# The first group of a cross-attention kernel: context turned through TensorE and ScalarE, and one unit's blocks moved per head

## What is computed

```
q = norm(x) @ Wq            # 16 heads of 128
k, v = ctx @ Wk, ctx @ Wv   # ctx: 2 x 2048 tokens x 128; 8 kv heads, each for 2 q heads
p = softmax(q k^T / sqrt(128), with a key mask)
x = x + (p @ v) @ Wo
```

## Time and profile before

| | |
|---|---|
| median of 3 runs | 354.47 us (354.44 to 355.21) |
| the profiled execution | 353.88 us |
| its span | 352.1 us |
| PE busy | 329.0 us, 93% |
| DVE, ACT, POOL busy | 278.7, 231.5, 244.9 us |

### The profile page before, as it was taken

One profiled execution on the slowest core, in us unless ns is written; L12 is line 12 of the kernel. 1 busy time (PEld: TensorE's weight loads), 2 busy tenths in 40 slices (PEclk: granted clock), 3 DMA queues, 4 the chain that ended last, 5 costly groups with the idle time before them and its releaser, 6 DMA issues.

```text
span 352.1 us, 6886 instructions
## 1 busy us (share of the span) xinstructions
PE 329.0 (93%) x2231; PEld 297.1 (84%) x2231; DVE 278.7 (79%) x472; ACT 231.5 (66%) x410; POOL 244.9 (70%) x150
## 2 busy tenths in 40 slices
PE   6875699999999999999999999998989999888996
PEld 4664599999999999999999988997878897588995
DVE  4599877988988989889889889735568844579997
ACT  4487577687677777777767687973246675257762
POOL 4839499599599599599598499778154868434550
PEclk9999989999999999999999999999999999999999
DMA  7705886886895895895795796693034040403630
GB/s 199 243 25 132 203 194 150 204 198 140 205 205 129 206 206 126 207 207 126 179 203 118 169 218 171 161 314 94 8 89 151 0 149 4 149 14 90 189 112 31
DMA packets 33332, 52.07 MB, mean 148 GB/s; under 512 B 5792, under 2 KB 23328, under 8 KB 33312
## 3 DMA queue, kind: packets, MB, share of 16 engines
q1 hardware_dynamic: 33312, 51.82, 58.9%
HBM read 20.08 MB, written 0.26 MB: 58 GB/s over the span
## 4 chain that ended last, share of the span: by engine, by line
PE 69%; DVE 8%; POOL 7%; issue 5%; ACT 4%; SPq 3%; DMA 3%; DVEq 0%; POOLq 0%; ACTq 0%
PE bank L554 11%; PE bank L555 11%; PE bank L556 10%; PE pair L554 10%; PE pair L556 10%; PE pair L555 10%; POOL pT L417 3%; POOL ctx_lo L417 3%; SPq L262 3%; DMA ctx_raw<-in_ctx_dram 2%; POOL ctxT_lo L417 2%; PE bank L801 1%; PE pair L793 1%; PE bank L832 1%; DVE resid L1680 1%
## 5 line engine op out<-in xcount | busy, mean ns | idle before, releaser
L417 POOL TENSOR_TENSOR pT<-pT,pT_hi 128x1024 fp32r<-128x1024 f32 x60 | 143.0, 2409 | 38.7 <-ACT pT_hi L1056 38.5
L1046 ACT ACTIVATE probs<-probs,lowest 128x2048 f32<-128x2048 f32 x32 | 64.2, 2007 | 23.6 <-DVE lowest L1366 23.5
L1056 ACT ACTIVATE pT_hi<-pT 128x1024 fp32r<-128x1024 f32 x60 | 61.6, 1052 | 16.2 <-DMA pT<-blocks 14.1
L555 PE MATMUL bank<-pT,ctx_hi 128*128 128x256 f32 x240 | 69.0, 288 | 0.0
L554 PE MATMUL bank<-pT_hi,ctx_lo 128*128 128x256 f32 x240 | 68.7, 286 | 0.0
L556 PE MATMUL bank<-pT_hi,ctx_hi 128*128 128x256 f32 x240 | 68.4, 285 | 0.0
L554 PE MATMUL pair<-ctxT_hi,qk_lo 128*128 128x512 f32 x128 | 51.7, 404 | 5.7 <-DVE qk_lo L1322 2.5
L1366 DVE CUSTOM_DVE_ANT_0 probs<-pair,mask_bias,lowest 128x1024 f32<-128x1024 f32 x32 | 41.0, 1281 | 12.7 <-PE pair L556 11.8
L556 PE MATMUL pair<-ctxT_hi,qk_hi 128*128 128x512 f32 x128 | 50.4, 394 | 0.0
L555 PE MATMUL pair<-ctxT_lo,qk_hi 128*128 128x512 f32 x128 | 50.3, 393 | 0.0
L554 PEld LDWEIGHTS bank<-pT_hi,ctx_lo 128*128 128x128 f32 x240 | 45.7, 191 | 1.5 <-POOL pT L417 0.5
(11 more groups left out here) (236 smaller groups left out, 810.8 us busy)
## 6 DMA issues: line engine op xcount, KB each, us to landing
pT<-blocks SPq DMA_DIRECT2D x128, 128.0 KB, 2.3
pT<-ctx_raw SPq DMA_DIRECT2D x112, 128.0 KB, 2.3
ctx_raw<-ffn_experts_gate_up_dram SPq DMA_DIRECT2D x16, 256.0 KB, 2.9
wq<-in_L_xattn_Wq_dram SPq DMA_DIRECT2D x8, 256.0 KB, 2.6
ctx_raw<-in_ctx_dram SPq DMA_DIRECT2D x8, 256.0 KB, 6.5
wo<-in_L_xattn_Wo_dram SPq DMA_DIRECT2D x8, 256.0 KB, 3.0
blocks<-in_L_attn_w_q_dram SPq DMA_DIRECT2D x4, 512.0 KB, 4.0
blocks<-in_L_attn_w_dense_dram SPq DMA_DIRECT2D x4, 512.0 KB, 4.4
```

Of the source, the lines that this page charges most:

```text
L417: pool.tensor_tensor(dst, src, hi.bitcast(F32), ALU.subtract).then_inc(ready, 1)
L555: pe.matmul(dst, w[0], x[1], start=False, stop=False)
L1046: act.activation(probs[:, j], probs[:, j], ACT.Exp, bias=lowest[:, p, j, 1:2], scale=-1.0, accum_out=den[:, p, j:j + 1]).then_inc(exps, 1)
L1056: act.activation(hi_slot(c), chunk(p, c).bitcast(F32), ACT.Copy).then_inc(pT_hi_ready, 1)
```

## The change

The turned context of p = 1 (chunks 4 to 7) is no longer made from the raw chunks with a DVE subtraction. ACT rounds the raw chunk, POOL takes its rest, then PE transposes the hi part and the lo part separately (`ctx_part`, eight pieces in the order of `PARTS`), and ACT copies each out of PSUM. For this, `ctx_round` of chunks 4 to 7 comes before that of 2 and 3, and POOL's rests become eight pieces of 512 columns, four of them ahead of `rest_wq(1)` and of the second mask. The second mask is loaded into the bytes of `wo`, so `load_o(0)` waits behind both masks and moves behind the moves of unit 0. `q_fold(0)` comes before the fourth chunk. In the first group the blocks of unit 0 move head by head: 16 DMAs of 32 rows x 2 KB for head 0 once it is turned, `load_wk(2)`, then 16 for head 1. The counts of `landed[0]` shift by 256.

```diff
+        PARTS = ((0, 0), (0, 1), (0, 2), (1, 0), (1, 1), (0, 3), (1, 2), (1, 3))
...
+        def move(eng, p, a, q, heads=slice(0, J)):
+
+            eng.dma_start(pT[p][LN * q:LN * (q + 1), a, heads].bitcast(F32),
+                          blocks[p][LN * a:LN * (a + 1), q, heads]).then_inc(landed[p], 16)
...
+            load_wq(1)
+            load_wk(1)
             load_mask(1)
-            load_o(0)
...
-            load_wq(1)
-            load_wk(1)
...
             load_wq(2)
-            move_blocks(0, 0)
-            load_wk(2)
+            for j in range(J):
+                sp.wait_ge(turned, j + 1)
+                for r in range(QD):
+                    for q in range(QD):
+                        move(sp, 0, q, (q + r) % QD, slice(j, j + 1))
+                if j == 0:
+                    load_wk(2)
+            sp.wait_ge(mask_ready, B * NCH)
+            load_o(0)
             load_wq(3)
...
+            def ctx_rest(b, k, rounded):
+                pool.wait_ge(ctx_hi_ready, rounded)
+                part, cols = slice(4 * k, 4 * k + 4), slice(b * KEYS + k * CH, b * KEYS + (k + 1) * CH)
+                rest(ctx_lo[:, b, part].rearrange("p i d -> p (i d)"), ctx_raw[:, cols],
+                     ctx_hi[:, b, part].rearrange("p i d -> p (i d)"), ctx_lo_ready)
...
             mask(0)
+            for k in range(NCH):
+                ctx_rest(1, k, 3 + k)
+            rest_wq(1)
             mask(1)
-            rest_wq(1)
-            ctx_rest(0)
-            ctx_rest(1)
+            for k in range(NCH):
+                ctx_rest(0, k, B * NCH)
...
+            def ctx_part(n):
+
+                lo, k = PARTS[n]
+                if lo:
+                    pe.wait_ge(ctx_lo_ready, k + 1)
+                else:
+                    pe.wait_ge(ctx_hi_ready, k + 3)
+                if n < 2:
+                    pe.wait_ge(ctxT_lo_ready, n + 3)
+                elif n == 2:
+                    pe.wait_ge(qk_lo_ready, 2)
+                else:
+                    pe.wait_ge(parts_ready, n - 2)
+                for i in range(4):
+                    last = pe.transpose(PART_BANK[n % 3][:, i * P:(i + 1) * P],
+                                        (ctx_hi, ctx_lo)[lo][:, 1, 4 * k + i].bitcast(F32), ident[:])
+                last.then_inc(parts_psum, 1)
...
+            score(0, 0)
+            ctx_part(0)
+            pe.wait_ge(ctxT_lo_ready, NCH)
+            score(0, 1)
+            ctx_part(1)
+            score(0, 2)
+            score(0, 3)
+            for n in range(2, 7):
+                ctx_part(n)
+            q_project(1, 0)
+            q_project(1, 1)
+            ctx_part(7)
+            pe.wait_ge(parts_ready, 5)
+            score(0, 4)
+            pe.wait_ge(parts_ready, 8)
+            score(0, 5)
+            wk_transpose(1)
...
             fold_copy(0, 1)
-            ctx_chunk(4)
-            ctx_chunk(5)
+            ctx_round(4)
+            ctx_round(5)
+            ctx_part(0)
+            ctx_part(1)
+            ctx_round(6)
+            ctx_round(7)
+            wq_round(1)
             exp_row(0, 0)
-            ctx_chunk(6)
-            ctx_chunk(7)
-            wq_round(1)
+            ctx_part(2)
+            ctx_part(3)
             exp_row(0, 1)
-            for c in range(1, B * NCH):
-                ctx_round(c)
+            for n in range(4, 8):
+                ctx_part(n)
+            ctx_round(2)
+            ctx_round(3)
```

More of the change, by code:

```diff
@@ L183, in perceiver_layer @@
         D_LAST = (bank[7], bank[1])
-        CTX_BANK = [bank[i] for i in (2, 3, 4, 5, 4, 5, 4, 5)]
+        CTX_BANK = [bank[i] for i in (2, 3, 4, 5)]
+        PART_BANK = bank[4:7]
+        PARTS = ((0, 0), (0, 1), (0, 2), (1, 0), (1, 1), (0, 3), (1, 2), (1, 3))
         TURN_BANK = [bank[i] for i in (7, 6, 0, 1, 7, 6, 0, 1)]
@@ L220, in perceiver_layer @@
         ctx_hi_ready, ctx_lo_ready = sem("ctx_hi_ready"), sem("ctx_lo_ready")
+        parts_psum, parts_ready = sem("parts_psum"), sem("parts_ready")
         wv_hi_ready, wv_ready, wo_hi_ready, wo_ready = (
@@ L258, in perceiver_layer @@
         stored = sem("stored")
-        def move(eng, p, a, q):
-            eng.dma_start(pT[p][LN * q:LN * (q + 1), a].bitcast(F32),
-                          blocks[p][LN * a:LN * (a + 1), q]).then_inc(landed[p], 16)
+        def move(eng, p, a, q, heads=slice(0, J)):
+            eng.dma_start(pT[p][LN * q:LN * (q + 1), a, heads].bitcast(F32),
+                          blocks[p][LN * a:LN * (a + 1), q, heads]).then_inc(landed[p], 16)
         block = stack.enter_context(nc.Block())
@@ L308, in _, with move_blocks @@
                          ).then_inc(ld_gate, 16)
-            load_wq(1)
-            load_wk(1)
-            def move_blocks(g, p):
+            def move_blocks(g, p, rounds=range(QD)):
                 after(sp, av, 4 * (2 * g + p - 1))
                 sp.wait_ge(turned, 2 * (2 * g + p) + 2)
-                for r in range(QD):
+                for r in rounds:
                     for q in range(QD):
@@ L338, in _ @@
                     load_o(g)
-            sp.wait_ge(landed[0], 256 * G)
+            sp.wait_ge(landed[0], 256 * (G + 1))
             def load_qkv(r):
@@ L689, in _ @@
             ctx_chunk(2)
+            q_fold(0)
             ctx_chunk(3)
[L691 to L705, removed]
+            pe.wait_ge(ctxT_lo_ready, 2)
+            score(0, 0)
[15 more added lines that the diff above has]
+            wk_transpose(1)
+            score(0, 6)
+            score(0, 7)
+            q_fold(1)
             for m in range(BEATS):
                 if m == 2:
-                    pe.wait_ge(ctx_lo_ready, 1)
-                if m == 6:
-                    pe.wait_ge(ctx_lo_ready, B)
+                    pe.wait_ge(ctx_lo_ready, B * NCH)
                 beat(1, m, True, False, True)
@@ L982, in ctx_chunk, with ctx_part @@
                 act.activation(ctxT_hi[:, b, k * CH:(k + 1) * CH], CTX_BANK[c][:], ACT.Copy).then_inc(ctxT_hi_ready, 1)
+            def ctx_part(n):
+                lo, k = PARTS[n]
+                act.wait_ge(parts_psum, n + 1)
+                act.activation((ctxT_hi, ctxT_lo)[lo][:, 1, k * CH:(k + 1) * CH], PART_BANK[n % 3][:],
+                               ACT.Copy).then_inc(parts_ready, 1)
             def ctx_round(c):
@@ L1052, in p_round @@
                 if c == 0:
[L1053 removed]
+                    act.wait_ge(landed[p], 256 * (g + 2 - p))
                 after(act, av, 4 * (u - 1) + c + 1 if not isinstance(u, int) or u else 0)
@@ L1115, in _ @@
             ctx_chunk(1)
+            ctx_round(1)
             ctx_chunk(2)
@@ L1375, in turn @@
                 if j == 0:
-                    after(dve, landed[p], 256 * g)
+                    after(dve, landed[p], 256 * (g + (0 if isinstance(g, int) and g == 0 else 1 - p)))
                 dve.transpose(blocks[p][:, :, j].rearrange("p q k t -> p k q t"),
@@ L1493, in _ @@
             ctx_chunk(3)
+            fold_rest(0, 1)
             dve.wait_ge(mask_ready, 2)
@@ L1497, in _ @@
             dve.wait_ge(mask_ready, 4)
[L1498 to L1507, removed]
+            for m in range(1, 4):
+                mask_pair(0, m)
             turn(0, 0)
             turn(0, 1)
+            dve.wait_ge(mask_ready, 6)
             mask_pair(0, 4)
+            dve.wait_ge(mask_ready, B * NCH)
             mask_pair(0, 5)
-            any_key(1)
             q_rest(1)
@@ L1517, in _ @@
             fold_rest(1, 0)
-            dve.wait_ge(ctxT_psum, B * NCH)
             dve.wait_ge(ctx_hi_ready, B * NCH)
-            dve.wait_ge(ctx_lo_ready, B)
+            dve.wait_ge(ctx_lo_ready, B * NCH)
             turn(0, 2)
             turn(0, 3)
+            for p in range(B):
+                any_key(p)
             group(1, True, False)
```

12 lines of the change are left out of this document (3 added, 9 removed).

## The result

The changed kernel takes 363.41 us (median of 4 runs, 362.67 to 363.70) against 354.46 for the kernel before in the same session: a ratio of 1.0249, interval 1.0216 to 1.0281. It is 9.0 us slower; the prediction said 5.3 slower and a range that ended at 361.5. The profiled execution took 362.67, its span is 360.9 instead of 352.1: +8.8 to be explained, where the sum said +5.6. It is the fastest of the four; the median lies 0.7 us above it, as 0.6 was forecast.

The account below looks back on a forecast made before the run. PE's own work bounds the kernel from group 1 on, so only group 0's delay counts: first attend 49.5 plus 1.7 slow clock, 51.2 against 45.5, is +5.6 on 353.9. Named: 359.8 us, range 352.0 to 361.5.

Parts of the forecast that it names:

- the sum: Whole kernel: first attend at 51.2 in full-speed terms against 45.5 before, +5.6 us.
- The step on which all hung: Unit 0's moves in group 0: 64 KB moves issue every 0.635 us, like 128 KB ones.
- T: Group 0: start of ACT's rounding of unit 0's blocks, 45.9 instead of 40.75; first attend 3.55 us later.
- The slow clock: PE's cold restart after its hole before the first attend: 1.7 us charged, the same as before.
- The end of unit 1: Second unit's moves: piece 0 ready at 61.7, before PE gets there at 63.3, so nothing is added.
- What the rebuild frees: Group 0, POOL, DVE and PE: context rests end at 32.0 instead of 36.0; PE could attend from 40.8.
- T = 26.25 + 31 s: Unit 0's moves start at 23.45; 32 issues at pitch s, 0.635 us, put ACT's rounding at 45.9.
- Nothing else in the diff touches a later group: Groups from 1 on: unaffected except for the order of two loads, which was taken to cost nothing.
- PE without holes from then on: Sign expected in the profile after: PE runs without a hole once past its first attend near 49.5.
- The full price: Unit 0's moves at a pitch of 0.59 to 0.64 us: +4.5 to +5.8, or 1.7 less if clock holds; chance 0.48.
- the late rebuild: Rival, group 0: ping-pong between PE and ACT turns head 0 a us late, +1 on any case; chance 0.06.

Follow-up runs that it names:

- the moves alone: The kernel before, with only the first unit's moves split by head; 363.68 us, ratio 1.0270.
- half the bytes: The changed kernel with only the first half of unit 0's key blocks moved in group 0, 32 moves of 32 KB; 361.43 us in one execution.
- whole moves: The changed kernel with unit 0's blocks moved as before, 16 moves of 128 KB; 353.83 us against 354.16, ratio 1.0004.
- two queues: The changed kernel with eight of head 1's moves issued by ACT instead of SP; 358.65 us in one execution.
- one turn written out on the changed kernel: The changed kernel with one turn of PE's loop (group 2) written out by hand, same work in more instructions; 364.57 us in one execution.
- two turns written out: The changed kernel with 128 KB moves, second mask in `ones`, and groups 2 and 3 of PE's loop written out; 351.93 us against 354.23, ratio 0.9932.

## Why the prediction was wrong, point by point

**Direction and main mechanism: right.** The step on which all hung, that 64 KB moves are issued at the pitch of 128 KB ones, is shown three times: 0.63 us each in the moves alone and at half the bytes, and the moves' whole time is cut only by a second issuing engine. From T to the first attend it is 51.26 - 47.72 = 3.54 us, as taken. The slow clock cost 1.5 us behind the first attend where 1.7 was charged; that this was close is in part luck, since the run of the moves alone paid 2.9 us after a hole of nearly the same length. The end of unit 1 added nothing.

**What the rebuild frees: right, but each step came about 1 us later.** POOL's last context rests ended at 33.1 (32.0 forecast), heads 2 and 3 were transposed from 33.99 to 38.4 (33.2 to 37.7), wk's transpose came at 40.20 (39.3). Score 2 ended at 42.0, when PE's hole begins (40.8). None of this was on the path that decided. With whole moves PE was through with score 2 at 41.3 and attended at 42.15, 3.3 us earlier than before, where the prediction's 40.8 would have made it 4.7.

**T = 26.25 + 31 s: the first step that failed, too small by 1.8 us.** T was 47.72, not 45.9. SP started at 24.40, not at 23.45. This start varies: it is 23.57, 23.45 and 23.47 in the runs with half the bytes, with two queues and with one turn written out on the changed kernel, and in those PE's wait for the context chunks was shorter too; so 0.9 us of it belong to this execution and not to the rebuild. How usual such a start is stays open, since the other three executions of the changed kernel were longer still. The other part is that s was taken as the same for all 32 moves: one issue of the first sixteen took 1.71 us instead of 0.59, at 28.2, with a q8 packet at 28.0 beside it (11.23 us for 16, but 10.00 for the next 16). The landing, 2.0 us instead of 2.2, gave 0.2 back. The earlier trace rows shows nothing of the kind, its longest issue is 0.708: in the kernel before that packet comes at 24.3, ahead of the first move at 28.73. The change starts the moves 4.3 us sooner, and its packet falls among them; in the three other runs named here the issue beside it took 1.13 to 1.45 us.

**"Nothing else in the diff touches a later group": the second step that failed.** It is true of the code and false of the time. The rebuild makes TensorE's program longer, which moves the fetch packet of the last groups from a unit where it cost 0.6 us to one where it cost 1.9: 1.3 us. This is shown by the run that writes out one turn in the kernel before (a hole appears), and by the one that writes out two (it goes); that the packet is TensorE's follows from these and from the matmul counts, not from a label in the trace. The sign "PE without holes from then on" failed with this step. The Trainium skill, Runtime: NRT & Kernel Launch, section Instruction fetch mechanics, says that each engine's sequencer streams its program by DMA in 16 KiB blocks and that crossing a block is mostly hidden. The size agrees with the 16 KB packets of q8 (those of q14 have 8 KB). That the crossing is hidden agrees for PE itself where the moves have slack: it is busy 27.00 of 27.00 us from 75 to 102 with a packet at 93.5. It is not hidden from the moves: one issue took 1.83 us there, and in the last group such a delay came back to PE as a hole.

**The sum again.** Forecast 5.6, and 1.8 for T, less 0.2 for the clock, is 7.2; the traces have 7.3 up to the last group. With 1.3 there it is 8.6, of the 8.8 by which the spans differ. The remaining 0.2 lie behind PE's last matmul and were not followed. The larger part of both failed steps is the same thing left out, an instruction packet among the moves: 1.1 us of the first and all 1.3 of the second.

**The chances.** The full price had 0.48. Its pitch came true; its price of +4.5 to +5.8 did not (at s = 0.59 the sum gives +4.3, not +4.5), for the two terms above. One rival had head 0 turned a us late, with 0.06, but by the rebuild's own work; the packets stand in none. The range ended at 361.5 because its upper bound took in only one late step of 1 us (the late rebuild) and no disturbed issue.

**Left open.** It isn't shown why the first chunks of the context landed later in the profiled execution of the changed kernel, nor why the version with two turns written out sometimes falls to the slow clock for 6.8 us in group 1 (its profiled execution did; its other runs' mean clock is 0.995 to 1.0). Nor is it shown why the clock stayed low for 5.8 us behind the first attend in the run of the moves alone and for 3.0 in the changed kernel. To have ACT issue all of head 1 was not tried.

## What to carry to other kernels

Where moves between partitions are issued one by one, count the issues and not the bytes: splitting a unit in two doubled its time, and only a second issuing engine bought some of it back. An edit of one stage is worth what it moves in the last wait of that stage, and it pays to follow the gain to the end of the trace: here 3.2 us were gained, and 1.2 lost one unit later, 1.1 of them to a load put ahead of the next moves. Where a later stage has little slack in its transfers, an edit that only lengthens a program can cost or gain over a microsecond there, so compare the last groups too before the edit itself is judged.

## What the runs showed of the hardware

- One SBUF-to-SBUF move of 32 rows holds its issuing engine for 0.59 us, 0.63 with the gap, at 128, 64 and 32 KB alike; SP and ACT issue side by side at that pitch each. The time to landing went from 2.3 us at 128 KB to 2.0 at 64 KB and 1.8 at 32 KB.
- A 16 KB instruction packet among such moves lengthened one issue, mostly to between 1.0 and 2.0 us, or, when it came behind the last issue, the landing of that move from 2.4 to between 3.5 and 4.0 us. PE stayed busy 27.00 of 27.00 us over one such packet; in the last groups one cost PE 0.6 us in one unit and 1.8 to 2.4 us in the next.
- After PE's hole of 9.28 us, with work resumed at 51.26, the clock stayed at its lower level until 54.3, 3.0 us on; with the hole at 8.28 us the slow stretch was as long, 10.2 us in all, but began later in the hole and lasted 5.8 us past its end.
